# Attention over sorted edges: three steps of VectorE's order moved between the raise of the maxima and the addition of the bias

## The chip, the cores and the metric

One core of a Trainium2 chip runs the kernel. The metric is device time in microseconds (us). TensorE is named PE in the profile, VectorE DVE, ScalarE ACT, GpSimd POOL and SyncE SP.

## The reference, cut to what matters

A graph has 12500 nodes with 128 features and 200000 edges, sorted by their destination. An attention layer comes first, then three graph convolutions with batch norms, each part with a residual. Only the attention is touched by the change:

```
h = relu(layernorm(x));  q, k, v = h Wq^T, h Wk^T, h Wv^T     # 8 heads of 16
scores = einsum(q[dst], k[src]) / sqrt(16) + edge_attr @ We^T  # the bias
ex     = exp(scores - segment_max(scores, dst)[dst])
out    = segment_sum(v[src] * ex / segment_sum(ex, dst)[dst], dst)
x      = x + out
```

## The kernel before

`attend` goes over the edges in 196 blocks of 1024 edges (8 columns of 128). The maximum, the sum of exponentials and the weighted sum of each node are kept in SBUF (`aux` and `state`) and are raised, scaled and added to block by block, at columns that a register names.

Each engine has a list of stages written out by hand (`steps`). In one iteration an engine runs every stage of its list once, each for the block that lies its lag behind. Engines wait for each other by semaphores only, and each engine keeps its own order strictly. The loop body holds four iterations.

- GpSimd (`gather`, L723): for each block eight indirect gathers (L730) fetch 128 rows of `kv_tab` each, by row numbers that lie in SBUF (`idx`). Behind each gather stands a small memset (L734), and the next gather waits for the memset before the last one. The buffers hold four blocks. A gather into one waits for `msg_made`, that is for `messages` of the block that was there.
- SyncE (`load`, L678): row numbers, edge attributes (L684) and the q rows (L690, eight DMAs), the last of these when `spread_q` of the iteration is through.
- VectorE (L874): the maxima of the scores over a run (`run_max`, L786), `own_max` (L795), `products` (L767, two halves, each waits for four gathers), `above_score` (L802), `scale_nodes` (L851), `node_max` (L815), `add_up` (L774), `shrink` (L863, L864), `raise_max` (L835, L836, L839), `add_bias` (L780), `merge` (L871, L872), `place_one` (L757), `hot_one` (L749), `messages` (L808), `fall_short` (L844).
- TensorE (L1015), around the change: `turn_near` (L950, needs `node_max`; `raise_max` needs it), `spread_q` (L941), `bias` (L1011; `add_bias` needs it), `turn_max` (L955), `turn_scores` (L963, needs `add_bias`), `give_back` (L978; `fall_short` needs it), `spread_scores` (L986; `run_max` of the next iteration needs it), `sum_up` (L898, needs `messages`). `put_nodes` (L929, L930), which `merge` needs, stands ahead of `turn_near`.
- ScalarE (L1095) casts the placing matrix (`cast_place`, L1080) behind its copy of the turned scores (`copy_scores`).

The operands of the stages that the change touches:

- `place_one` compares a broadcast column with a row of node numbers; both inputs are in SBUF.
- `hot_one` does the same for the 16 destinations of a run; both inputs are in SBUF.
- `merge` adds two PSUM results to `state` and `aux`; one input of each is in SBUF.
- `messages` multiplies the gathered v rows by the exponentials, 128x1024 elements; both inputs are in SBUF.
- `add_bias` adds the PSUM bias to the sums of products.

Of the kernel before, what the change touches and what calls it, by code (L numbers as in the profile page):

```python
# [568 lines left out]
def attend(nc, sh, env):  # L569

    ident, state, aux = env["ident"], env["state"], env["aux"]
    with ExitStack() as c:
# [166 lines left out]
        def _(dve):  # L739
# [4 lines left out]
            with passes(dve, sh, env) as w:  # L744
# [121 lines left out]
                def merge(s):  # L866
# [7 lines left out]
                steps(dve, sh.BLOCKS, SLOTS, [  # L874
                    (3, run_max(0)), (3, run_max(1)), (3, own_max), (2, products), (3, above_score),
                    (4, scale_nodes), (4, load_bases), (3, node_max), (2, add_up), (3, load_first), (4, shrink),
                    (3, raise_max), (2, add_bias), (4, merge), (0, place_one), (0, hot_one),
                    (3, messages), (3, fall_short)], w)
                dve.wait_ge(added, 2 * (w + 1) * sh.BLOCKS)
                next_pass(nc, dve, sh, env, (turn, wrap, by, step), (moved, tables), w)  # L880

# [1719 lines left out]
```

## Time and profile before

| | us |
|---|---|
| median of 3 runs | 6202.45 (6200.96 to 6206.25) |
| the profiled execution: its time | 6205.67 |
| the profiled execution: its span | 6203.9 |
| mean granted TensorE clock in it | 0.766 |
| busy in the span: PE, DVE, POOL, ACT | 5259.4, 4526.3, 4496.4, 2295.7 |

The span is what the profiler recorded from the first to the last instruction; the time of that execution is 1.8 us longer. The attention's blocks lie between 219 and 2773 us of the span. Busy shares over the whole span mix this stage with others and don't tell what limits it; the rows further down are of this stage alone.

### The profile page before, as it was taken

The page shows a single profiled execution, that of the slowest core. Times are in us where ns is not written, and L with a number is a line of the kernel's source. Part 1 is how long each engine was busy: PE and PEld are TensorE (multiplying, and loading weights), DVE is VectorE, ACT ScalarE, POOL GpSimd, SP SyncE. Part 2 cuts the span into 40 slices and gives each one's busy share as a digit, 9 for nine tenths or more (in the row PEclk, how much of TensorE's full clock was granted, in tenths as well). Part 3 has the DMA queues.
Part 4 walks back from the last instruction along what each step waited for, and adds up shares of the span by engine and source line. Part 5 has one row for each costly group of instructions (what it writes and reads, how often), then busy time and mean ns, then how long its engine had stood idle before and what let it go on. Part 6 is the DMA issues. An engine that isn't in the chain of part 4 may idle for free. (4 is left out here: it accounts for less than half of the span.)

```text
span 6203.9 us, 165021 instructions
## 1 busy us (share of the span) xinstructions
PE 5259.4 (85%) x49582; PEld 3541.0 (57%) x49582; DVE 4526.3 (73%) x13500; ACT 2295.7 (37%) x5686; POOL 4496.4 (72%) x6062
## 2 busy tenths in 40 slices
PE   3688888888888888874799699998899997699995
PEld 2355555555555555553577467675476765467674
DVE  7566666666666666668899688886488887788886
ACT  3333333333333333333344244443644443444442
POOL 2588888888888888867000198886298886588883
PEclk9655565555555655555677699999999999899997
DMA  4433333333333333324333443333433334533335
GB/s 134 137 100 99 100 99 99 99 99 100 99 98 100 99 99 99 99 80 134 110 92 95 122 117 112 112 117 99 136 113 114 114 112 106 179 112 114 114 111 163
DMA packets 542000, 688.39 MB, mean 111 GB/s; under 512 B 217072, under 2 KB 427905, under 8 KB 541722
## 3 DMA queue, kind: packets, MB, share of 16 engines
q0 software_dynamic: 140208, 338.71, 19.8%
q1 hardware_dynamic: 401692, 348.45, 18.8%
q8 instruction: 49, 0.80, 0.1%
q14 instruction: 51, 0.42, 0.0%
HBM read 619.25 MB, written 67.52 MB: 111 GB/s over the span
## 5 line engine op out<-in xcount | busy, mean ns | idle before, releaser
L730 POOL DMA_INDIRECT at_kv<-kv_tab,at_idx x1568 | 1541.5, 983 | 276.6 <-POOL at_rest L734 139.6
L2247 ACT ACTIVATE ag_msg<-ag_pair 128x768 bf16<-128x768 f32 x1200 | 944.2, 809 | 1371.1 <-PE ag_pair L2177 1298.5
L2186 PE MATMUL ag_sum<-ag_hot,ag_msg 128*128 128x240 bf16 x10800 | 1267.4, 267 | 1.1 <-DVE ag_msg L2116 0.7
L2186 PEld LDWEIGHTS ag_sum<-ag_hot,ag_msg 128*128 128x128 bf16 x10800 | 982.9, 98 | 334.0 <-issue 287.6
L2058 POOL DMA_INDIRECT ag_spill<-g_tab,ag_idx x600 | 587.2, 979 | 687.0 <-DMA ag_idx<-spill_tab 578.5
L2099 DVE TENSOR_SCALAR ag_hot<-iota_win,ag_node 128x240 bf16<-128x240 bf16 x4350 | 994.4, 339 | 0.0
L2067 POOL DMA_INDIRECT ag_spill<-g_tab,ag_idx x750 | 731.1, 975 | 126.3 <-POOL ag_rest L2070 80.9
L2177 PE MATMUL ag_pair<-xs,ag_pick 128*32 128x384 bf16 x14400 | 758.9, 330 | 67.3 <-issue 62.9
L734 POOL MEMSET at_rest<- 8x448 f32 x1568 | 723.2, 461 | 0.1
L2116 DVE CAST ag_msg<-ag_pair 128x768 bf16<-128x768 f32 x600 | 570.2, 950 | 131.5 <-PE ag_pair L2177 104.8
L2177 PEld LDWEIGHTS ag_pair<-xs,ag_pick 128*32 128x32 bf16 x14400 | 301.0, 96 | 330.0 <-issue 214.7
L767 DVE TENSOR_TENSOR at_prod<-at_ps_q,at_kv 128x512 f32<-128x512 f32 x392 | 271.1, 692 | 263.3 <-DMA at_kv<-kv_tab,at_idx 220.4
L2089 DVE TENSOR_SCALAR ag_pick<-ag_pick,iota_p 128x1024 bf16<-128x1024 bf16 x450 | 248.2, 552 | 263.4 <-DMA ag_pick<-slot_tab 259.7
L786 DVE TENSOR_REDUCE at_ml<-at_ps_bc 128x4 f32<-128x512 f32 x392 | 252.5, 686 | 219.6 <-issue 111.3
L986 PE MATMUL at_ps_bc<-at_sct,at_sel_head 64*128 64x128 f32 x3136 | 406.7, 437 | 0.7 <-issue 0.5
L2070 POOL MEMSET ag_rest<- 8x448 f32 x750 | 381.5, 509 | 0.0
L986 PEld LDWEIGHTS at_ps_bc<-at_sct,at_sel_head 64*128 64x128 f32 x3136 | 349.2, 324 | 6.2 <-issue 1.2
L906 PE MATMUL at_ps_scale<-at_scale,at_sel_feat 8*128 8x128 f32 x392 | 121.8, 401 | 264.5 <-DVE at_above L802 211.7
L2061 POOL MEMSET ag_rest<- 8x448 f32 x600 | 308.3, 514 | 0.0
L941 PE MATMUL at_ps_q<-at_qd,at_hot_b 64*128 64x512 bf16 x1176 | 283.3, 616 | 13.9 <-DVE at_prod L767 9.4
L1011 PEld LDWEIGHTS at_ps_scale<-at_we,at_attr 128*128 128x128 f32 x784 | 181.2, 321 | 162.1 <-issue 155.6
L1034 ACT ACTIVATE at_below<-at_above 128x64 f32<-128x64 f32 x196 | 50.2, 256 | 581.8 <-DVE at_above L802 465.5
(333 smaller groups left out, 9313.9 us busy)
## 6 DMA issues: line engine op xcount, KB each, us to landing
ag_pick<-slot_tab SPq DMA_DIRECT2D x150, 768.0 KB
rk_hi_bc<-hi_tab SPq DMA_DIRECT2D x50, 896.0 KB
at_attr<-attr SPq DMA_DIRECT2D x196, 128.0 KB
at_qd<-q_tab SPq DMA_DIRECT2D x1568, 12.0 KB
at_kv<-kv_tab,at_idx POOLq DMA_INDIRECT x1568
ag_spill<-g_tab,ag_idx POOLq DMA_INDIRECT x1350
tr_dv<-dinv_tab SPq DMA_DIRECT2D x72, 256.0 KB
g_tab<-xs SPq DMA_DIRECT2D x48, 384.0 KB
```

The lines of the kernel that those rows point to most:

```text
L730: nc.gpsimd.indirect_dma_start(kv[:, s.slot, ch, :], None, env["kv_tab"], bass.IndirectOffsetOnAxis(ap=idx[:, s.slot, ch:ch + 1], axis=0)) ...
L734: nc.gpsimd.memset(rest[:, ch % 2, :], 0.0).then_inc(rested, 1)
L986: last = nc.tensor.matmul(ps_bc[j][:, h * P:(h + 1) * P], sel_head[own, h, :], sct[own, s.slot % 2, :], start=False, stop=h == HALF - 1, s ...
L2058: nc.gpsimd.indirect_dma_start(spill[:, k, o, :], None, table, bass.IndirectOffsetOnAxis(ap=idx[:, k, o:o + 1], axis=0)).then_inc(tail_in[ ...
L2061: nc.gpsimd.memset(rest[:, (k + o) % 2, :], 0.0).then_inc(rested, 1)
L2067: nc.gpsimd.indirect_dma_start(spill[:, k, o, :], None, table, bass.IndirectOffsetOnAxis(ap=idx[:, k, o:o + 1], axis=0)).then_inc(spill_in ...
L2070: nc.gpsimd.memset(rest[:, (k + o) % 2, :], 0.0).then_inc(rested, 1)
L2099: last = nc.vector.tensor_scalar(hot[:, k, ch, :], env["iota_win"][:, :], node[:, k, ch:ch + 1], None, ALU.is_equal)
L2116: nc.vector.tensor_copy(msg[:, p % 4, :, :], pair_ps[p % 3][:, :, 0:3 * DIM]).then_inc(copied[p], 1)
L2177: last = nc.tensor.matmul(pair_ps[p % 3][at, ch % 2, 0:3 * DIM], pick[:, k, ch * P + j * CAP:ch * P + (j + 1) * CAP], xs[:, (P // CAP) * c ...
L2186: last = nc.tensor.matmul(sum_ps[k][:, 0:WIN], row[:, part * DIM:(part + 1) * DIM], hot[:, k, ch, :], start=first and part == 0, stop=end ...
L2247: nc.scalar.activation(msg[:, p % 4, :, :], pair_ps[p % 3][:, :, 0:3 * DIM], ACT.Copy).then_inc(copied[p], 1)
```

## The change

On VectorE alone, `place_one`, `hot_one` and `merge` are put between `raise_max` and `add_bias`, in that order. Before, they stood behind `add_bias`, as `merge`, `place_one`, `hot_one`. What follows `add_bias` is now `messages`. Lags, waits, buffers and operands are the same, and so are the other engines' lists.

```
                 (3, run_max(0)), (3, run_max(1)), (3, own_max), (2, products), (3, above_score),
                 (4, scale_nodes), (4, load_bases), (3, node_max), (2, add_up), (3, load_first), (4, shrink),
-                (3, raise_max), (2, add_bias), (4, merge), (0, place_one), (0, hot_one),
-                (3, messages), (3, fall_short)], w)
+                (3, raise_max), (0, place_one), (0, hot_one), (4, merge), (2, add_bias), (3, messages),
+                (3, fall_short)], w)
```

## Rows read from the trace of the kernel before

**Rows 1.** Windows: stretch, length, busy (x instructions) of five engines, clock, DMA share, GB/s.
```profile
219.00:2749.00 2530.00, 2144.32 (x12839) 1354.14 (x12839) 1620.21 (x4075) 776.31 (x3110) 2257.68 (x3135) 0.58 0.36 99
```
**Rows 2.** GpSimd's groups there: operation, count, busy us, mean ns, idle before by cause.
```profile
L730 POOL DMA_INDIRECT at_kv<-kv_tab,at_idx x1568 | 1541.5, 983 | 276.6 <-POOL at_rest L734 139.6 <-issue 136.9
L734 POOL MEMSET at_rest<- 8x448 f32 x1567 | 722.7, 461 | 0.1
```
**Rows 3.** GpSimd's timeline, one cycle: start us, us, line, operation, [idle before].
```profile
999.55 0.95 POOL L730 DMA_INDIRECT at_kv<-kv_tab,at_idx  x1 [0.16 <-POOL at_rest L734]
...
1001.12 1.23 POOL L730 DMA_INDIRECT at_kv<-kv_tab,at_idx  x1 [0.16 <-issue]
...
1002.96 0.95 POOL L730 DMA_INDIRECT at_kv<-kv_tab,at_idx  x1 [0.16 <-issue]
...
1007.68 0.95 POOL L730 DMA_INDIRECT at_kv<-kv_tab,at_idx  x1 [0.16 <-POOL at_rest L734]
```
**Rows 4.** VectorE over the same cycle, by time.
```profile
999.11 0.22 DVE L780 TENSOR_TENSOR at_sc<-at_qk,at_ps_scale 128x64 f32<-128x64 f32 x1 [1.42 <-PE at_ps_scale L1011]
999.25 0.29 DVE L871 TENSOR_TENSOR state<-state,at_ps_node 128x128 f32 x1
...
1000.30 1.22 DVE L808 TENSOR_TENSOR at_msg<-at_kv,at_msg 128x1024 f32<-128x1024 f32 x1
...
1006.24 0.69 DVE L767 TENSOR_TENSOR at_prod<-at_ps_q,at_kv 128x512 f32<-128x512 f32 x1 [0.92 <-DMA at_kv<-kv_tab,at_idx]
...
1007.42 1.21 DVE L774 TENSOR_REDUCE at_qk<-at_prod 128x64 f32<-128x1024 f32 x1
...
1010.32 0.28 DVE L839 TENSOR_TENSOR aux<-aux,at_mnew 8x128 f32 x1
1012.02 0.22 DVE L780 TENSOR_TENSOR at_sc<-at_qk,at_ps_scale 128x64 f32<-128x64 f32 x1 [1.42 <-PE at_ps_scale L1011]
```
**Rows 5.** GpSimd: gathers that met L808, one long, and the last of 111.
```profile
1065.26 1.84 POOL L730 DMA_INDIRECT at_kv<-kv_tab,at_idx  x1 [0.16 <-issue]
...
2731.75 1.59 POOL L730 DMA_INDIRECT at_kv<-kv_tab,at_idx  x1 [0.16 <-POOL at_rest L734]
```
**Rows 6.** VectorE's L808 beside these two.
```profile
1065.06 1.22 DVE L808 TENSOR_TENSOR at_msg<-at_kv,at_msg 128x1024 f32<-128x1024 f32 x1
...
2731.29 1.22 DVE L808 TENSOR_TENSOR at_msg<-at_kv,at_msg 128x1024 f32<-128x1024 f32 x1
```
**Rows 7.** TensorE before and behind the addition of the bias, by time.
```profile
1008.62 0.60 PE L930 MATMUL at_ps_node<-at_place,at_nodes 128*9 128x128 f32 x2
...
1013.11 0.60 PE L978 MATMUL at_ps_max<-at_m_node,at_place_t 128*128 128x8 f32 x2
```
**Rows 8.** VectorE's bias addition over the stage: waits before it.
```profile
L780 DVE TENSOR_TENSOR at_sc<-at_qk,at_ps_scale 128x64 f32<-128x64 f32 x195 | 43.1, 221 | 270.2 <-PE at_ps_scale L1011 267.5 <-issue 2.8
```
**Rows 9.** GpSimd's timeline: a gap, and two eighth gathers of later phase.
```profile
533.74 1.04 POOL L730 DMA_INDIRECT at_kv<-kv_tab,at_idx  x1 [1.22 <-issue]
...
810.60 0.95 POOL L730 DMA_INDIRECT at_kv<-kv_tab,at_idx  x1 [0.16 <-issue]
...
977.53 0.95 POOL L730 DMA_INDIRECT at_kv<-kv_tab,at_idx  x1 [0.16 <-issue]
```
**Rows 10.** VectorE around these two, and around 1020 us.
```profile
806.32 0.22 DVE L780 TENSOR_TENSOR at_sc<-at_qk,at_ps_scale 128x64 f32<-128x64 f32 x1 [1.42 <-PE at_ps_scale L1011]
...
813.86 0.69 DVE L767 TENSOR_TENSOR at_prod<-at_ps_q,at_kv 128x512 f32<-128x512 f32 x1 [1.44 <-DMA at_kv<-kv_tab,at_idx]
...
973.21 0.22 DVE L780 TENSOR_TENSOR at_sc<-at_qk,at_ps_scale 128x64 f32<-128x64 f32 x1 [1.41 <-PE at_ps_scale L1011]
...
980.36 0.69 DVE L767 TENSOR_TENSOR at_prod<-at_ps_q,at_kv 128x512 f32<-128x512 f32 x1 [0.81 <-DMA at_kv<-kv_tab,at_idx]
...
1018.79 0.69 DVE L767 TENSOR_TENSOR at_prod<-at_ps_q,at_kv 128x512 f32<-128x512 f32 x1 [0.66 <-DMA at_kv<-kv_tab,at_idx]
...
1024.01 0.22 DVE L780 TENSOR_TENSOR at_sc<-at_qk,at_ps_scale 128x64 f32<-128x64 f32 x1 [1.31 <-PE at_ps_scale L1011]
```

## The prediction

> **What bounds the kernel now.** I read the busy table by stages first, then GpSimd's groups, then the waits, and last the timelines of GpSimd and VectorE side by side. The stretch of the attention's blocks lasts 2530 us. In it PE is busy for 2144 us, DVE for 1620 us and POOL for 2258 us [rows 1]. None is full by that count, but POOL's is deceptive. Its time is the gathers (mean 0.983 us), the memsets (0.461 us) and the idle time before gathers [rows 2]. That idle time is 0.16 us nearly everywhere [rows 3]; it is 1.2 us at some 16 places of 1568, such as the one at 533.74 us [rows 9]. So POOL never waits for another engine. A gather that nothing disturbs takes 0.952 us, and gathers follow each other at 0.95 + 0.46 + 0.16 = 1.57 us. Eight make a block: 12.57 us. The cycle of VectorE from 999.11 to 1012.02 us is 12.91 us long [rows 4], and 196 cycles of that are the stage. POOL's stream sets the pace, and VectorE waits for it: the second half of the products ends its wait when the eighth gather has landed [rows 4].
>
> The 0.34 us between 12.57 and 12.91 are the subject. The gather at 1001.12 us took 1.23 us instead of 0.95 [rows 3]. It began while `messages` ran (1000.30 to 1001.52 us) and ended 0.83 us after it [rows 4]. The gather at 1065.26 us took 1.84 us and ended 0.82 us after its `messages`; so did the last of 111 such gathers, which began 0.46 us into it and took 1.59 us [rows 5, 6]. The reader is to see that `messages` holds a gather that meets it: a gather begun between some 0.05 and 1.08 us after the start of `messages` ends 1.22 + 0.82 = 2.04 us after that start, whenever it began. In all this costs 1568 x (0.983 - 0.952) = 49 us [rows 2]. A tensor reduction of the same length, 1.21 us at 1007.42 us, holds nothing: the gather at 1007.68 us took 0.95 us [rows 3, 4].
>
> A page of the Trainium skill, "SBUF — State Buffer", section "Who interferes with whom", says that a VectorE instruction with two SBUF inputs contends with a GpSimd instruction that reads SBUF; the gather reads its row numbers there, and by that rule the trace agrees. The same section of the Trainium skill infers that `tensor_tensor` does not stall descriptor generation, which needs the write port. By that inference nothing here would be held, and the change would be worth nothing; the 1.84 us gather speaks against it.
>
> **The phase.** Why does the held time stay at about 0.3 us a cycle? Because VectorE and POOL lock. Count from the start A of `add_bias` (999.11). `messages` starts at A + 1.19 [rows 4]. The gather held by it ends at A + 1.19 + 2.04 = A + 3.23. The next one, which is the eighth of its block (1002.96 us), ends 1.57 later, at A + 4.80 [rows 3]. The second half of the products starts 2.33 us after that end, at 1006.24 us, and the next `add_bias` 5.78 us after it, at 1012.02 us [rows 4]. Sum: 4.80 + 2.33 + 5.78 = 12.91. The held time is what is left over 12.57: 0.34 us. It is not POOL's choice; it follows from where `messages` stands.
>
> **The change, part by part.** Removed from behind `add_bias`: `merge`, `place_one`, `hot_one`. `messages` started 1.19 us after A. It will start where `merge` does now, 0.14 us after A [rows 4]: its exponentials and rows have long been there. It moves 1.05 us ahead.
>
> Added ahead of `add_bias`: the same instructions, four of them, in a wait. The wait is 270.2 / 195 = 1.39 us on average [rows 8]. From the first of them to `messages` it is 1000.30 - 999.25 = 1.05 us [rows 4]. `raise_max` ends at 1010.60 us, so they would be through by about 1011.65 us, and the bias is added at 1012.02 us. So the addition is not later, with some 0.35 us to spare. Without that cover they would cost at most 1.05 us a block. `merge` brings its wait for `put_nodes` along, ahead of the bias. What is queued behind it is `add_bias`, and TensorE's scores behind that. `put_nodes` ends at 1009.22 us [rows 7], 1.4 us before, so this wait is free. The direct yield of the move is nothing too. `place_one`'s reader on ScalarE stands behind the copy of the scores, and TensorE reads the one-hot after `spread_scores`. `fall_short` needs `give_back`, which ends at 1013.71 us [rows 7], and the next maxima wait for `spread_scores`. VectorE only idles 1.05 us longer there. No DMA is issued by VectorE; SP's queue is passed by nothing. `shrink` and `raise_max` don't move.
>
> What is late next, then, is the eighth gather. The held gather now ends at A + 0.14 + 2.04 = A + 2.18. If it is again the seventh, the eighth ends at A + 3.75, lands 2.33 us later at most as the rows show, at A + 6.08, and the cycle would be 6.08 + 5.78 = 11.9 us. POOL can't do eight gathers in that, so the gathers fall back until the held one is the sixth. The eighth then ends at A + 2.18 + 3.14 = A + 5.32. The new cycle is 5.32 + landing + 5.78.
>
> The landing is the cost that I have to bound. Behind a gather that ends at A + 4.80 it is 2.33 us. At 977.53 us an eighth gather ended 5.27 us after A (973.21) and the products began 1.88 us later; at 810.60 us one ended 5.23 us after A (806.32), and they began 2.31 us later [rows 9, 10]. With 1.88 the cycle is 12.98 and 0.41 is held; with 2.31 it is 13.41, held 0.84. Of the gathers that end as late or later, most are like the first. I take 2.03: 13.13 us, 0.56 held.
>
> Not all cycles are so. In 52 of 193 the bias comes earlier than 5.7 us after the products, as at 1024.01 us, 5.22 us after 1018.79 [rows 10]. There `messages` comes before its gather and holds it for about 0.1 us. Sum over the stage: 142 x 0.56 + 52 x 0.1 = 85 us held, against 49 now: 36 us more. `place_one` and `hot_one` have two SBUF inputs like `messages` and may hold a gather for their 0.3 us at most; in their new place, 1.4 us ahead of the bias, the gathers of the new cycle start at A - 2.3 and A - 0.7 and miss them: 0. The 16 gaps stay. The blocks after the last gather and all other stages stay. The start of `messages` could be 0.1 us later than `merge` starts now, which adds 0.1 x 142 = 14 us; I put 3 us in for it. Together +39 us.
>
> On the profiled execution: 6205.7 + 39 = 6245 us. That execution lies 3.2 us above the median of the three runs; against the median it is 6202.45 + 39 = 6241 us. The forecast's own range is +14 (landing 1.88: 142 x 0.41 + 5 - 49) to +80 us.
>
> **The rivals.**
> - *Late landings.* Every eighth gather lands after 2.31 us: 142 x 0.84 + 5 - 49 = +75 us, 6278 us. For it: the row at 810.60 us. Against it: the row at 977.53 us.
> - *The cover is too thin.* If the four instructions take 0.2 us more than the gap, the bias is 0.2 us late in each cycle, and since the cycle runs through the bias, 0.2 x 194 = 39 us come on top: 6280 us. It decides from 0.35 us more than I count. Against it: 1.42 us of gap before nearly every L780.
> - *Nothing.* The phase of gathers and `messages` wanders instead of locking, as much is held as before, and the time stays at 6202 us. For it: most gathers are undisturbed now, and the held ones vary, by 0.28 us at 1001.12 and by 0.89 us at 1065.26 [rows 3, 5]. The inference of the Trainium skill's page above ends here too.
> - *Faster, the other side.* The stream slips into a lock without a hold. The eighth gather ends between A + 3.8 and A + 4.15 (behind `messages`, not in it), and its landing takes over 12.57 - 5.78 - 4.15 = 2.64 us because it runs together with the q rows. Then no gather is held, up to 49 us go, 6154 us. It decides from a landing of 2.64 us. Against it: the longest of these rows is 2.33.
>
> **How the numbers follow.** Forecast 0.55, late landings 0.13, thin cover 0.08, nothing 0.14, faster 0.10. A measurement of this kernel tells about 0.2% (12 us) from no change. The first three are slower: 0.76. Time 6241 us. The range goes from 6198 us, which takes in "nothing", to 6290 us, above the late landings; it leaves out the faster case and combinations of two slower ones.
>
> **What would show it.** GpSimd's gathers in the stage: mean 0.983 us now, 0.983 + 36 / 1568 = 1.006 us after, with the memsets and the 0.16 us unchanged; more gathers of 1.4 to 1.8 us, none before the sixth. `messages` 0.14 to 0.2 us behind `add_bias`, and the cycle between two `add_bias` at 13.1 us. The wait before L780 falls from 1.42 to 0.2 to 0.4 us and its start stays 5.78 us behind the second half of the products; if that distance grows, the cover is too thin. The time outside 219 to 2773 us equal. I am wrong if the mean gather is at 0.983 us or below, or if POOL's idle time before gathers grows.

## The result and the profile after

The changed kernel takes 6254.5 us (median of 4 runs, 6252.48 to 6260.42) beside 6204.35 us before (4 runs): ratio 1.0082, 95% interval 1.0065 to 1.0100, some 50 us slower. Forecast were 6241 us and a loss of 39. Two executions of the experiments further down lie far above the others of their kernels (6364.82 us of kernel 1, 7555.16 us of kernel 4) and are not in the ratios given there.

The profiled execution took 6252.48 us with a span of 6250.7 us. From the start of the first gather to the start of the last `merge` it is 2604.5 us (2553.2 before); all else together is 4.5 us shorter. So the whole difference lies in the attention's blocks. The window and GpSimd's groups of the changed kernel, which answer to [rows 1] and [rows 2]:

```profile
219.00:2749.00 2530.00, 2104.94 (x12584) 1325.75 (x12584) 1587.88 (x3995) 762.40 (x3051) 2261.89 (x3073) 0.59 0.35 98
```
```profile
L730 POOL DMA_INDIRECT at_kv<-kv_tab,at_idx x1568 | 1590.0, 1014 | 277.4 <-POOL at_rest L734 160.0 <-issue 117.4
L734 POOL MEMSET at_rest<- 8x448 f32 x1568 | 724.5, 462 | 0.1
```

The window is the same stretch of time, but the changed kernel is not through with its gathers at its end (the last one begins at 2798.3 us, before at 2748.1), so the busy times of its other engines are of fewer blocks. GpSimd's groups take in all of them. The granted clock of TensorE over the window is 0.59, and 0.58 before, so it doesn't explain the loss. Memsets and idle time are what they were; the gathers alone grew, from 983 to 1014 ns. 1590.0 - 1541.5 = 48.5 us, against 51.0 us by which the stream from the first to the last gather lengthened. GpSimd's timeline of one cycle of the changed kernel, for [rows 3]:

```profile
1160.10 1.67 POOL L730 DMA_INDIRECT at_kv<-kv_tab,at_idx  x1 [0.16 <-POOL at_rest L734]
...
1162.39 0.95 POOL L730 DMA_INDIRECT at_kv<-kv_tab,at_idx  x1 [0.16 <-POOL at_rest L734]
...
1163.96 0.95 POOL L730 DMA_INDIRECT at_kv<-kv_tab,at_idx  x1 [0.16 <-issue]
...
1173.41 1.50 POOL L730 DMA_INDIRECT at_kv<-kv_tab,at_idx  x1 [0.16 <-POOL at_rest L734]
```

And VectorE's, for [rows 4]:

```profile
1159.58 0.22 DVE L780 TENSOR_TENSOR at_sc<-at_qk,at_ps_scale 128x64 f32<-128x64 f32 x1 [0.35 <-PE at_ps_scale L1011]
1159.72 1.22 DVE L808 TENSOR_TENSOR at_msg<-at_kv,at_msg 128x1024 f32<-128x1024 f32 x1
...
1166.95 0.69 DVE L767 TENSOR_TENSOR at_prod<-at_ps_q,at_kv 128x512 f32<-128x512 f32 x1 [1.20 <-DMA at_kv<-kv_tab,at_idx]
...
1171.04 0.28 DVE L839 TENSOR_TENSOR aux<-aux,at_mnew 8x128 f32 x1
1171.37 0.29 DVE L757 TENSOR_TENSOR at_place<-off,iota_n 128x128 f32<-128x128 f32 x1
1171.58 0.28 DVE L749 TENSOR_TENSOR at_hot<-rel,iota_w 128x128 bf16<-128x128 f32 x1
1171.78 0.28 DVE L871 TENSOR_TENSOR state<-state,at_ps_node 128x128 f32 x1
1172.09 0.29 DVE L872 TENSOR_TENSOR aux<-aux,at_ps_node 9x128 f32 x1
1172.73 0.22 DVE L780 TENSOR_TENSOR at_sc<-at_qk,at_ps_scale 128x64 f32<-128x64 f32 x1 [0.35 <-PE at_ps_scale L1011]
```

Read them together; A is again the start of `add_bias`, here 1159.58 us. `messages` starts 0.14 us after A. The gather of 1160.10 us meets it 0.38 us in and takes 1.67 us; it ends 2.05 us after the start of `messages`. It is the sixth: the eighth (1163.96) ends 5.33 us after A, the second half of the products begins 2.04 us later, the next addition 5.78 us after that. Cycle 13.15 us, forecast 13.13. The moved instructions fit: the wait before L780 is 0.35 us.

### The profile page after: what moved, and what is told of

Its sections match the earlier page's. It is cut to its first block and busy times, and to the rows that moved or that the text cites. A ratio compares the mean times of both kernels' runs of the same rounds, so it can differ in the third digit from the quotient of the medians.

```text
span 6250.7 us, 165021 instructions
## 1 busy us (share of the span) xinstructions
PE 5258.2 (84%) x49582; PEld 3535.3 (57%) x49582; DVE 4521.7 (72%) x13500; ACT 2298.2 (37%) x5686; POOL 4544.7 (73%) x6062
## 5 line engine op out<-in xcount | busy, mean ns | idle before, releaser
L730 POOL DMA_INDIRECT at_kv<-kv_tab,at_idx x1568 | 1590.0, 1014 | 277.4 <-POOL at_rest L734 160.0
```

Source lines behind the costliest of these rows:

```text
L730: nc.gpsimd.indirect_dma_start(kv[:, s.slot, ch, :], None, env["kv_tab"], bass.IndirectOffsetOnAxis(ap=idx[:, s.slot, ch:ch + 1], axis=0)) ...
```

## The experiments

My theory: `messages`, with two SBUF inputs, holds the gather that meets it, and where it starts after the addition of the bias sets for how long. Rival A: the work put ahead of the addition costs by itself. Rival B: the compares (`place_one`, `hot_one`) hold the gathers in their new place. "Stage" is the stretch from the first gather to the last `merge` in the profiled execution, of which there is one for each kernel. "Kernel 3" is that of experiment 3. On the chips of the first eight kernels single executions of one kernel differ by up to 1.4% (6226.11 to 6311.13 us for the kernel before). The changed kernel was profiled twice, here and in experiment 5: the spans differ by 36 us, the stages by 5. So for kernels 1 to 8 the stage and the mean gather say more than the total, and a difference of 5 us in the stage is no more than what a repeat shows.

**1 and 2. One input of `messages` from PSUM, in both orders**

```
+        ex_ps = ps_node[:, 160:224].rearrange("p (c h) -> p c h", h=HEADS)
...
+                    s.freed(act, msg_made, 1)
+                    s.freed(act, nodes_made, 1)
+                    nc.scalar.activation(ex_ps, below..., ACT.Exp, ...)
...
-                    ex = msg[:, k % 2, :, DIM:DIM + HEADS].unsqueeze(2).to_broadcast([P, C, HC, HEADS])
+                    ex = ex_ps.unsqueeze(2).to_broadcast([P, C, HC, HEADS])
```

ScalarE writes the exponentials a second time, into PSUM, and waits for `messages` of the block before (`s.freed`); VectorE's `messages` then reads them there. Lines behind the added one count one more, so the gather is L731 and `messages` is L809.

> The order of before, but `messages` reads the exponentials from PSUM (ScalarE writes them there once more), so that it has one SBUF input instead of two. Theory (`messages` holds the gather that meets it because both of its inputs lie in SBUF, and where it stands after the addition of the bias sets how long): no gather is held by it, the 49 us of held time before go but for a few us by the smaller instructions, some 6160 us; mean gather 0.955 us. Rival A (VectorE's order costs by itself, through the bias addition and TensorE): the gathers don't matter, 6202 us or, since `messages` may take 0.15 us longer and ScalarE has one instruction more, up to 30 us slower. Rival B (`place_one` and `hot_one` are what holds gathers): 6202 us.

> The same with the changed order. Theory: once `messages` holds nothing, the order doesn't matter: equal to the previous kernel within 6 us, some 6160 us, that is 95 us under the changed kernel. Rival A: it stays some 50 us above the previous kernel. Rival B: the same 50 us, from the two compares in their new place.

Measured: ratio to before 0.9941 (0.9899 to 0.9982) in the old order, 0.9926 (0.9895 to 0.9958) in the changed one. Stage 2511.1 and 2517.8 us. GpSimd's gathers in the two, old order first:

```profile
L731 POOL DMA_INDIRECT at_kv<-kv_tab,at_idx x1568 | 1497.5, 955 | 277.4 <-issue 180.3 <-POOL at_rest L735 97.1
```
```profile
L731 POOL DMA_INDIRECT at_kv<-kv_tab,at_idx x1568 | 1496.3, 954 | 277.4 <-issue 189.6 <-POOL at_rest L735 86.6 <-DVE at_msg L809 1.2
```

In the old order one gather that meets `messages`, GpSimd's and VectorE's timelines:

```profile
1008.99 0.95 POOL L731 DMA_INDIRECT at_kv<-kv_tab,at_idx  x1 [0.16 <-issue]
```
```profile
1008.66 1.22 DVE L809 TENSOR_TENSOR at_msg<-at_kv,at_ps_node 128x1024 f32<-128x1024 f32 x1
```

It starts 0.33 us into `messages`, where by the 2.04 us it would take 1.7 us with two SBUF inputs, and takes 0.95. It is not alone: 131 gathers of kernel 1 and 169 of kernel 2 begin while `messages` runs, and none of them takes over 1.0 us. In the kernel before 113 of 164 such gathers did, in the changed kernel 170 of 180. The hold is gone though `messages` is as long as before, and with it the cost of the order: from the first gather to the last it is 2486.7 and 2484.6 us, and the median cycle is 12.57 and 12.58 us, which is eight undisturbed gathers. Kernel 2's stage is 6.7 us longer all the same, a little over the 6 us that I had allowed; that lies behind its last gather. Rivals A and B, which wanted 50 us between the two, fall.

**3 and 4. Half of the move**

```
3:  (3, raise_max), (4, merge), (2, add_bias), (0, place_one), (0, hot_one), (3, messages)
4:  (3, raise_max), (0, place_one), (0, hot_one), (2, add_bias), (4, merge), (3, messages)
```

> Only `merge` is put ahead of the addition of the bias; the two compares stay behind it, so `messages` starts 0.55 us after it (1.19 before, 0.14 in the changed kernel). Theory: the eighth gather ends at 0.55 + 2.04 + 3.14 = 5.73 us after the addition, the landing of 1.9 and 5.78 make a cycle of 13.4, 0.85 held in each ordinary cycle: slower than either, +60 to +80 us, 6262 to 6285 us, though only half of the instructions have moved. Rival A: the cost goes with the work put ahead (0.64 of 1.05 us): about +30 us. Rival B: compares unmoved, so no change, 6203 us.

> Only `place_one` and `hot_one` are put ahead of the addition of the bias; `merge` stays behind it, so `messages` starts 0.78 us after it. Theory: a gather held there ends 2.82 us after the addition, the eighth ends at 4.4 to 4.8, which with a landing of 2.3 and 5.78 closes the cycle at 12.6 us without a hold: 0 to 15 us faster than before, 6188 to 6203 us. Rival A: +20 us, 6223 us. Rival B: the whole loss of the changed kernel, +50 us, 6253 us.

Measured: ratios 1.0012 (0.9981 to 1.0044) and 0.9983 (0.9951 to 1.0015). Stage 2576.6 us (+23) and 2553.0 us (0), mean gather 997 and 982 ns. Kernel 4 falls at the edge of what the theory gave; its hold is not gone, for 61 of 195 eighth gathers still end 6.0 us after the addition. In kernel 3 I placed `messages` wrongly: `place_one` starts 0.34 us behind the start of the addition, where I had counted the 0.14 us of `merge`, so `messages` came 0.75 us behind the addition, not 0.55. (Both begin with an empty instruction; why `place_one` comes later isn't shown.) Two locks are then open. In 77 of 195 cycles the eighth gather ends 5.9 or 6.0 us after the addition, with 0.7 us held on average (up to 1.07) and 13.7 us to the next addition. In 104 others it ends at 4.4 to 4.9, with 0.06 us held and 12.4 us to the next addition. The place and size that I expected were missed; in kernel 3 alone +23 would fit rival A's +30 as well, but that rival wanted +20 in kernel 4, and experiments 5 to 7 separate them further. The totals of both kernels are within noise of the kernel before.

**5, 6 and 7. The changed kernel again, with idle work, and one compare ahead**

```
6:  +                    nc.vector.tensor_reduce(idle[:, :], prod[:, 0:HALF, :].rearrange(...), AX.X, ALU.add)
6:  (3, raise_max), (0, place_one), (0, hot_one), (4, merge), (2, add_bias), (2, pause), (3, messages)
7:  (3, raise_max), (0, place_one), (2, add_bias), (4, merge), (0, hot_one), (3, messages)
```

> The changed kernel once more, for its attention stage on this chip beside the next three. Theory: the phase is fixed by the instruction order, so the stage from the first gather to the last `merge` is 2604 us again within 5 (2553 in the kernel before), the mean gather 1.01 us, and `messages` holds the sixth gather of some 160 blocks. Rival (the phase wanders from run to run): anything from 2530 to 2610 us, mean gather 0.96 to 1.02.

> The changed kernel with one more instruction: between the addition of the bias and `messages` VectorE reduces 128x512 elements of the products into a tile that nothing reads (about 0.6 us; one SBUF input). Theory: only the start of `messages` counts. It comes 0.8 us behind the addition, as in the kernel with the compares ahead, so the same stage: 2545 to 2560 us, 50 us FASTER than the changed kernel by more work; mean gather 0.98 us. Rival (VectorE's or TensorE's chain carries the loss): 196 x 0.6 us more work can't help: 2604 us or up to 120 us more.

> Only `place_one` is put ahead of the addition of the bias; `messages` starts 0.98 us behind it. Theory: the gather held there ends 3.02 us after the addition, the eighth at 4.6 us; with a landing of 2.1 to 2.3 and 5.78 the cycle closes at 12.57 with next to no hold, and it is farther from the double lock at 5.9 us than the kernel with both compares ahead: stage 2535 to 2548 us, mean gather 0.97 us, 5 to 18 us faster than before. Rival (the cost goes with the work put ahead): 10 us slower than before, stage 2563 us.

| | ratio to before (95%) | `messages` after A, us | mean gather, ns | stage, us |
|---|---|---|---|---|
| 5 changed again | 1.0079 (1.0054 to 1.0104) | 0.14 | 1017 | 2609.6 |
| 6 changed + idle work | 1.0039 (1.0009 to 1.0070) | 0.73 | 997 | 2578.0 |
| 7 `place_one` ahead | 1.0000 (0.9974 to 1.0025) | 1.02 (mean) | 979 | 2547.6 |

The phase repeats: 5 has its stage 5.1 us from the first run's, and the sixth gather is held in 152 blocks (162 there). Kernel 6 does more work on VectorE in each block, 0.68 us, and its stage is 32 us shorter than that of kernel 5, with a mean gather 20 ns shorter. That is against a theory in which the added work costs by itself. The gain is read from one profile of each kernel: the totals (medians 6298.88 us in kernel 6, 6303.55 in kernel 5) don't show it, as their intervals overlap. The expected 50 us weren't reached. `messages` came at 0.73 and not 0.8 us, and as in kernel 3 there are two locks: 79 cycles with the eighth gather at 5.9 us and 0.7 us held on average. Kernel 7 gained 6 us in the stage, hardly more than a repeat differs by, and nothing measurable in the total.

**8. Shorter memset between gathers**

```
-        rest = tile("rest", [HEADS, 2, REST])
+        rest = tile("rest", [HEADS, 2, 320])
```

> The kernel before with the small memset between gathers cut from 448 to 320 elements, for the claim that GpSimd's stream paces the stage. It writes zeros that nothing reads. Theory: the memset falls from 0.46 to 0.33 us, eight gathers from 12.57 to 11.5 us, less than the shortest cycle that VectorE and TensorE can run (11.95: 5.5 + 0.69 + 5.78). The cycle falls to 12.0 to 12.3 us, the stage from 2553 to 2380 to 2430 us, and the products no longer wait for the eighth gather. Rival (VectorE or TensorE paces the stage at 12.9 us, and the gathers only fit themselves in): 2553 us, with GpSimd waiting for `messages` instead.

Ratio 1.0718 (1.0661 to 1.0775): some 445 us slower instead of 120 to 170 faster. Both expectations missed the time; of the rival, that GpSimd waits for `messages` came. GpSimd's gathers, VectorE around one pair of products, and TensorE's row for the maxima:

```profile
L730 POOL DMA_INDIRECT at_kv<-kv_tab,at_idx x1568 | 1501.1, 957 | 932.2 <-DVE at_msg L808 681.1 <-issue 198.7 <-POOL at_rest L734 52.4
```
```profile
1506.36 1.29 DVE L767 TENSOR_TENSOR at_prod<-at_ps_q,at_kv 128x512 f32<-128x512 f32 x2 [0.15 <-issue]
1510.05 0.22 DVE L802 TENSOR_TENSOR at_above<-at_sc,at_ps_scale 128x64 f32<-128x64 f32 x1 [2.40 <-remote]
```
```profile
1506.75 0.53 PE L911 MATMUL at_ps_scale<-at_md,at_hot_t 128*128 128x64 f32 x2
```

GpSimd runs as far ahead as its four buffers let it and waits for them; the products wait no more; but now `above_score` waits 2.4 us for the spread maxima of TensorE, and the cycle is 15.3 us. TensorE's row for that matmul ends at 1507.28 us, its semaphore rises at 1510.03. (The ends of TensorE's rows are modelled by the profile; the rise of the semaphore is recorded.) Such a distance between row and semaphore is 2.8 us in the median cycle here, and 0.3 us in the kernel before, 1.0 us in kernel 1, and 2.0 and 2.5 us in kernels 12 and 11 further down. So TensorE finishes the later behind its modelled rows, the less the gathers hold the loop back. The granted clock doesn't tell it (0.57 and 0.59 of full over 300 to 2700 us, here and before). Why is open.

**9 to 12. How far the stream can be quickened**

The tile above with 416 elements in the old order (9) and the changed one (10), with 384 in the old order (11), and 416 with the PSUM input (12; there ScalarE's second exponential stands behind `copy_count`, and `put_nodes` waits for it).

> The kernel before with the memset between gathers cut from 448 to 416 elements (0.461 to 0.434 us by the slope of the run with 320). Eight undisturbed gathers take 12.36 us instead of 12.57. Theory (products and `messages` lock to the stream): the eighth gather follows the held one 1.55 instead of 1.57 us later, so an ordinary cycle falls by 0.03 us only, and `messages` holds the gather 0.19 us longer; only the quarter of the cycles that aren't locked gains the full 0.21. Stage from the first gather to the last `merge` 2553 - 15 = 2538 us, mean gather up from 0.983 to 1.00. Rival (no lock, gathers pace alone): stage 2553 - 42 = 2511 us, mean gather unchanged. Third: the slow regime of the run with 320 elements (cycle 15.3 us) sets in here already: stage over 2600 us, and GpSimd waits for `messages`.

> The changed kernel with the same 416 elements. Theory: two gathers lie between the held one and the landing that closes the cycle, so an ordinary cycle falls by 0.05 us: stage 2607 - 19 = 2588 us, mean gather 1.03 us. Rival (no lock): 2565 us. Third: slow regime, over 2650 us.

> The kernel before with 384 elements (0.408 us, eight gathers 12.15 us). Theory: 2553 - 30 = 2523 us, mean gather 1.02 us, as long as the products still wait for the eighth gather. Rival (the slow regime begins where GpSimd gets ahead of the products): the unlocked cycles let it run ahead, the products stop waiting for gathers, and the cycle grows towards 15.3 us: stage 2700 to 3000 us. I hold the theory for somewhat likelier.

> A try at a faster kernel: order of before, `messages` reads the exponentials from PSUM, ScalarE's second writing of them stands behind its copy of the counts, and the memset has 416 elements. Theory: nothing is held and nothing locks, so the whole 0.21 us a cycle show: stage 2511 - 42 = 2469 us, total 80 us under the kernel before. Rival: with 448 elements the products had already stopped waiting for the gathers in that kernel (they began 5.4 us after the eighth on average), so GpSimd runs further ahead and TensorE's slow regime takes over: stage above 2511 us, GpSimd waits for `messages`.

| | median, us (before: 6205.23) | ratio (95%) | mean gather, ns | stage, us |
|---|---|---|---|---|
| 9 | 6186.04 | 0.9969 (0.9959 to 0.9980) | 995 | 2528.4 |
| 10 | 6221.4 | 1.0023 (1.0011 to 1.0034) | 1024 | 2577.8 |
| 11 | 6444.82 | 1.0384 (1.0350 to 1.0419) | 966 | 2796.1 |
| 12 | 6328.84 | 1.0198 (1.0154 to 1.0241) | 954 | 2691.6 |

9 and 10 show the lock as forecast in kind. In 9 the memsets are 42 us shorter in all (680.8 us against 722.7), of which longer gathers take 18 back (1559.7 against 1541.5), so that the stage gains 25; I had said 15. 10 gained 27 to 32 on the two profiled executions of the changed kernel, where I had said 19. 11 and 12 are the slow regime, against what I held likelier in 11. In both GpSimd waits for `messages`; here is its row for 11:

```profile
POOL at_kv L730 <- DVE at_msg L808: 356.0, 137, 3.7
```

Kernel 9 is faster than the kernel before (0.3%) and the changed one. Removing the hold and shortening the memset don't add up: each alone gains, together they let GpSimd get ahead. That the hold acts there as a part of the brake is argued, not shown. Kernel 12 also differs from kernel 1 in where ScalarE's second exponential stands and in the wait of `put_nodes` for it, and that form wasn't run with 448 elements, so these may have a part in its loss.

## Why the prediction was right, point by point

- *POOL's stream sets the pace.* It never waits for another engine, before or after; its idle time is 276.6 and 277.4 us. Right, with the limit that experiments 8, 9 and 11 set: with two SBUF inputs in `messages` the stream can be quickened by 0.2 us a block (416 elements), not by 0.4 (384) or 0.85 (320), where TensorE's results come later.
- *`messages` holds gathers, with 2.04 us from its start to the gather's end.* Shown by experiments 1 and 2; 2.05 us in the changed kernel. By the Trainium skill's page "SBUF — State Buffer", section "Who interferes with whom", two SBUF inputs contend with a GpSimd instruction that reads SBUF: the trace agrees. The inference there that `tensor_tensor` leaves descriptor generation alone can't be carried over to these indirect gathers: with one input in PSUM the mean gather is 954 ns against 1014 in the changed order, 955 against 983 in the old one. Which part of a gather waits, the reading of its row numbers or the making of its descriptors, no trace here shows.
- *`messages` moves to A + 0.14, the moved instructions are covered.* 0.14 us; 0.35 us of wait left, as worked out.
- *The sixth gather is held, the eighth ends at A + 5.32.* It ends at A + 5.33, in 161 of 195 cycles.
- *Landing 2.03 us.* 2.05 on average. The 2.03 was a choice between two rows, 1.88 and 2.31, which lie 61 us apart in the sum (142 x 0.43); that it came within 0.02 us is partly luck. The cycle: 13.13 forecast, 13.18 on average.
- *142 cycles of 0.56 us and 52 of 0.1.* This is the mis-sized term. Held time in all is 97 us, not 85: 1568 x (1.014 - 0.952). 196 gathers take over 1.0 us (132 before), 162 of them sixth ones. By cycles, 144 ordinary ones hold 84 us, 0.58 each, near the forecast 0.56. The 51 in which the bias comes early hold 13 us, 0.25 each and not 0.1. The trace before had this already: by the same count it has 59 such cycles, not 52, with 0.26 us each. With 97 the sum gives 97 - 49 = +48 us, against 50 measured. The 3 us put in for a later start of `messages` measured nothing.
- *The rivals.* Late landings, a thin cover and "nothing" didn't come. The faster lock was tried from the other side: no position of `messages` that I tried (0.14, 0.73, 0.75, 0.78, 1.02 and 1.19 us behind the addition) is free of holds.

Still open: why TensorE's results come later when the loop isn't braked by the gathers.

## What to carry to other kernels

An engine that is off the critical path and whose instructions have two SBUF inputs can slow a GpSimd that generates gathers; look at the spread of the gathers' durations before moving such work, and ask which gather it will meet. Where a stream and a loop wait for each other, cost isn't the sum of work: a later start can be cheaper than an earlier one, and idle work shortened the stage here by 32 us. A free slot ahead of a wait isn't a gain if nobody waits for what comes out of it.

## What the runs showed of the hardware that I had not expected

- A two-input compare of 128x128 elements holds a gather too, mostly by 0.13 us at most. In kernel 1, where `messages` holds nothing, GpSimd's gather that begins 0.03 us after `hot_one` (L750) takes 1.08 us instead of 0.95:

```profile
1388.66 1.08 POOL L731 DMA_INDIRECT at_kv<-kv_tab,at_idx  x1 [0.16 <-POOL at_rest L735]
```
```profile
1388.63 0.28 DVE L750 TENSOR_TENSOR at_hot<-rel,iota_w 128x128 bf16<-128x128 f32 x1
```

- Reading one of the inputs from PSUM cost `messages` nothing: 1.22 us either way.
- The small memset behind each gather is a brake that pays down to a point: with 416 instead of 448 elements the kernel is 0.3% faster, but with 384 it is 3.8% slower and with 320 7.2%.
